# Attention on one core: the score products of two steps made together, with their low-key part on 64-row tiles

## The chip, the cores and the metric

The kernel runs on one core of one Trainium2 chip. The metric is the device time of one launch in microseconds; lower is better. A profiled execution is taken by the hardware profiler, and its page and trace are what is read here.

## The reference

The program is a small transformer layer in float32: half of a mixture-of-experts layer is added to x, then an attention block, then half of the same mixture-of-experts layer again. The change touches only the attention, with 4 sequences of 1024 tokens, width 256, 16 heads of 64:

```python
q = (_ln(x, lnq_s, lnq_b) @ Wq + bq).reshape(Bq, Sq, H, HD).transpose(0, 2, 1, 3)
k = ...   # the same with Wk, bk
v = ...
scores = jnp.einsum('bhqd,bhkd->bhqk', q, k) / SMAX
mask = jnp.triu(jnp.full((Sq, Sq), -999.0), k=Sq - 1)
p = jax.nn.softmax(scores + mask, axis=-1)
att = jnp.einsum('bhqk,bhkd->bhqd', p, v)
```

(Bq = 4, Sq = 1024, H = 16, HD = 64.)

## The kernel before

The whole program is one block in which each engine runs its own instruction stream, written out by hand, and the streams meet in semaphores. It has four phases: `ffn_phase`, `attention_phase`, `mlp_phase` and `ffn_phase` again. Float32 precision is kept by splitting each operand into a high and a low part in the type fp32r, and by multiplying the parts.

`attention_phase` works in steps. One step handles one tile of 128 queries of one head against all 1024 keys. Eight steps make a head, 16 steps a pair of heads (a "slot"), and 32 steps one iteration of the loop; 16 iterations make 512 steps. In step k of an iteration the engines do this:

- TensorE (PE), in `on_tensor`: four score matmuls into `sc[:, k % 2]` (L1675); then eight 128x128 transposes into `tr` of the tile of three steps ago (L1687); then four matmuls into `ov` for the values (L1711), which run seven steps behind the scores; then, where there is one, half of a projection piece, three matmuls' worth into `pj` (L1622, L1629), which makes queries, keys or values for a later slot.
- VectorE (DVE), in `on_vector`: where a block of values has ended, a copy to `half` (L1569); then the row maximum of the scores (L1578), in one step of eight after one small operation for the mask (L1575); the reciprocal of the last step's sum (L1583); and two subtractions that write the low part of the transposed probabilities into `pT` (L1589).
- ScalarE (ACT), in `on_scalar`: where a block has ended, a copy to `ao` (L1414); two copies that write the high part of the transposed probabilities (L1421); the exponential with its row sum (L1427); and, where there is a projection piece, a copy to `staged` (L1382, L1379).
- GpSimd (POOL), in `on_gpsimd`: the scaling by the reciprocal (L1505) and the splitting of staged queries, keys and values into parts (L1458 to L1484).

The plan `AT` puts a piece at the odd steps 1, 3, 5, 9, 17, 19, 21, 23, 25, 27, 29 and 31. Its first half runs in the even step ahead of it, so that the pairs of steps (0,1), (2,3), (4,5), (8,9) and all pairs from (16,17) have projections in both steps, and the pairs (6,7), (10,11), (12,13) and (14,15) have none. A block of values ends after every fourth step, so that `half` and `ao` are written in the steps 3, 7, 11, ... (the odd step of every second pair).

The scores of one step: `q_s[:, slot, head]` holds the high part of the head's queries on 64 partitions and the low part on the other 64. `k_s[:, slot, head, 0]` holds the high part of the keys on both halves, and `k_s[:, slot, head, 1]` the low part on both halves; the second half is written by a DMA on the SP queue (`double_k`, L1261). Two matmuls over all 128 rows, one for each of the two k parts, so give all four products for 512 keys, and four give a step's tile. `sc` has room for two tiles. Ahead of its score matmuls a step waits for the exponential of the tile of two steps ago (`pe.wait_ge(s["exp"], u - 1)`), which frees the place.

Of the kernel before, what the change touches and what calls it, by code (L numbers as in the profile page):

```python
# [20 lines left out]
F32 = mybir.dt.float32  # L21
# [1070 lines left out]
def attention_phase(nc, turns, tag, w, zT, w_split, bias, att):  # L1092
# [34 lines left out]
    q_s = m.sb("q_s", [P, 2, 2, S], F32R, room=rooms.first)  # L1127
    k_s = m.sb("k_s", [P, 2, 2, 2, S], F32R, room=rooms.first)
    pT = m.sb("pT", [P, 2, 2, QT, BT], F32R, room=rooms.wide)
# [100 lines left out]
    def after(it):  # L1230

        return (it + 1) % NIT

    def on_sync(sp, ahead):
# [23 lines left out]
        def double_k(slot):  # L1258

            for head, (a, b) in enumerate(((0, HD), (HD, 0))):  # L1260
                sp.dma_start(k_s[b:b + HD, slot, head].bitcast(F32), k_s[a:a + HD, slot, head].bitcast(F32))\  # L1261
                    .then_inc(s["k_dup"], 16)

        def double_first(part):
            cols = slice(part * BT, part * BT + BT)
            for head, (a, b) in enumerate(((0, HD), (HD, 0))):
                sp.dma_start(k_s[b:b + HD, 0, head, :, cols].bitcast(F32), k_s[a:a + HD, 0, head, :, cols].bitcast(F32))\
                    .then_inc(s["k_dup"], 16)
# [36 lines left out]
        def body(it, first, last):  # L1305
# [13 lines left out]
            if not ends(it):  # L1319
                sp.wait_ge(s["split"], before(it, PAIR_UP))  # L1320
                load_wqk(after(it), 0)
                load_z(after(it))
            else:
                sp.wait_ge(s["split"], before(it, PAIR_UP))
                ahead["loads"]()
            store(it, 0, it * 2 + 1)
# [6 lines left out]

            sp.wait_ge(s["split"], before(it, QUERIES_UP))
            load_wqk(after(it), 1)
            sp.wait_ge(s["split"], before(it, ITER))
# [6 lines left out]
        sp.wait_ge(s["z_in"], 32 * NIT)  # L1343
        sp.wait_ge(s["k_dup"], 32 * 2 * NIT + 32)
        sp.wait_ge(f["res_out"], NB * 16 + 16)
# [5 lines left out]
    def parts_of(kind, part, slot, pair_slot):  # L1351

        cols = slice(part * BT, part * BT + BT)
        r0, r1 = rows_of_head(0), rows_of_head(1)
        if kind == "Q":
            hi = [q_s[r0, pair_slot, 0, cols], q_s[r1, pair_slot, 1, cols]]
            lo = [q_s[r1, pair_slot, 0, cols], q_s[r0, pair_slot, 1, cols]]
        else:
            hi = [k_s[r0, pair_slot, 0, 0, cols], k_s[r1, pair_slot, 1, 0, cols]]
            lo = [k_s[r0, pair_slot, 0, 1, cols], k_s[r1, pair_slot, 1, 1, cols]]  # L1360
        return (staged[r0, slot], staged[r1, slot]), hi, lo

    def on_scalar(act, ahead):
# [80 lines left out]
    def on_gpsimd(pool, ahead):  # L1444
# [42 lines left out]
        for n, (kind, part) in enumerate(FIRST):  # L1487
# [8 lines left out]
            else:  # L1496

                (x0, _), hi, _ = parts_of(kind, part, n % 2, 0)
                pool.wait_ge(s["staged"], n + 1)
                pool.tensor_scalar(hi[0], x0, 1.0, 1.0, ALU.mult, ALU.mult).then_inc(s["head0_hi"], 1)  # L1500

# [103 lines left out]
    def on_tensor(pe, ahead):  # L1605
# [42 lines left out]
        def body(it, first, last):  # L1648
            for k in steps(last):
                u = it * ITER + k  # L1650
                slot, head, tile = k // STEPS, (k // QT) % 2, k % QT
                if not last:
# [5 lines left out]
                    if k % STEPS == 0:  # L1658

                        pe.wait_ge(s["k_dup"], it * 64 + slot * 32 + 64)  # L1660
                        if slot:
# [6 lines left out]
                    if first and k == 4:  # L1668
                        pe.wait_ge(s["first_split"], 4)
                    if not (first and k < 2):  # L1670

                        pe.wait_ge(s["exp"], u - 1)
                    for kb in range(S // BT):
                        for a in range(2):
                            o = pe.matmul(sc[:, k % 2, kb * BT:(kb + 1) * BT],  # L1675
                                          q_s[:, slot, head, tile * P:(tile + 1) * P],
                                          k_s[:, slot, head, a, kb * BT:(kb + 1) * BT],
                                          start=(a == 0), stop=(a == 1))
                    o.then_inc(s["sc"], 1)
                if transposes_at(k, first, last):  # L1680
# [588 lines left out]
```

## Time and profile before

| | us |
|---|---|
| median of 3 runs | 2418.85 (2418.18 to 2421.43) |
| the profiled execution's own time | 2419.73 |
| its span | 2417.9 |
| PE busy | 2377.2 (98%) |
| DVE busy | 1865.4 (77%) |
| ACT busy | 1680.0 (69%) |
| POOL busy | 1516.2 (63%) |

The attention takes the stretch from about 285 us to about 1965 us of the span. Busy time of PE is modelled: a matmul's record lasts longer than the distance to the next one, since they are pipelined. The distance from the start of one group of matmuls to the start of the next is the time that the group takes of PE.

### The profile page before, as it was taken

The page shows a single profiled execution, that of the slowest core. Times are in us where ns is not written, and L with a number is a line of the kernel's source. Part 1 is how long each engine was busy: PE and PEld are TensorE (multiplying, and loading weights), DVE is VectorE, ACT ScalarE, POOL GpSimd, SP SyncE. Part 2 cuts the span into 40 slices and gives each one's busy share as a digit, 9 for nine tenths or more (in the row PEclk, how much of TensorE's full clock was granted, in tenths as well). Part 3 has the DMA queues.
Part 4 walks back from the last instruction along what each step waited for, and adds up shares of the span by engine and source line. Part 5 has one row for each costly group of instructions (what it writes and reads, how often), then busy time and mean ns, then how long its engine had stood idle before and what let it go on. Part 6 is the DMA issues. An engine that isn't in the chain of part 4 may idle for free.

```text
span 2417.9 us, 46347 instructions
## 1 busy us (share of the span) xinstructions
PE 2377.2 (98%) x14512; PEld 2066.7 (85%) x14512; DVE 1865.4 (77%) x3615; ACT 1680.0 (69%) x2932; POOL 1516.2 (63%) x1536
## 2 busy tenths in 40 slices
PE   8999999999999999999999999999999999999999
PEld 7888878888888888888888888888888889988888
DVE  7887687888878788887878878788887875466775
ACT  4555677877878787787878878787787864443443
POOL 1333378787777877778787777878778754542220
PEclk9999999999999999999999999999999999999999
DMA  4744631322212232131223212122221345332332
GB/s 181 263 165 157 209 114 44 101 75 78 96 44 87 61 96 83 56 96 44 87 72 93 96 37 94 44 98 76 78 96 44 109 170 174 122 119 71 126 126 80
DMA packets 131970, 245.67 MB, mean 102 GB/s; under 512 B 7290, under 2 KB 90132, under 8 KB 120052
## 3 DMA queue, kind: packets, MB, share of 16 engines
q1 hardware_dynamic: 131828, 244.15, 30.9%
q8 instruction: 44, 0.72, 0.1%
q14 instruction: 98, 0.80, 0.1%
HBM read 140.12 MB, written 53.67 MB: 80 GB/s over the span
## 4 chain that ended last, share of the span: by engine, by line
PE 83%; DVE 7%; issue 4%; POOL 3%; DMA 2%; ACT 1%; SPq 0%; DVEq 0%; POOLq 0%; ACTq 0%
PE a_ov L1711 20%; PE a_sc L1675 19%; PE a_tr L1687 19%; PE a_pj L1622 7%; PE a_pj L1629 4%; PE g_acc L964 3%; PE g_hid L922 3%; PE f_acc L964 2%; PE f_hid L922 2%; PE m_proj L2125 1%; POOL m_zin L1971 1%; PE m_hid L2194 1%; DMA f_xin<-in_x 1%; DVE f_hp L736 1%; DVE f_gated L731 1%
## 5 line engine op out<-in xcount | busy, mean ns | idle before, releaser
L1578 DVE TENSOR_REDUCE a_nmax<-a_sc 128x1 f32<-128x1024 f32 x512 | 626.5, 1224 | 251.9 <-PE a_sc L1675 248.1
L1421 ACT ACTIVATE a_pT<-a_tr 128x512 fp32r<-128x512 f32 x1024 | 559.5, 596 | 317.2 <-PE a_tr L1687 307.7
L1505 POOL TENSOR_SCALAR a_pr<-a_pr,a_rden 128x1024 f32<-128x1024 f32 x512 | 576.3, 1127 | 283.4 <-DVE a_rden L1583 212.8
L1589 DVE TENSOR_TENSOR a_pT<-a_tr,a_pT 128x512 fp32r<-128x512 f32 x1024 | 649.2, 675 | 18.7 <-ACT a_pT L1421 18.7
L1711 PE MATMUL a_ov<-a_pT,a_v_s 128*128 128x512 f32 x2032 | 594.2, 414 | 1.6 <-DVE f_zT L778 1.2
L1427 ACT ACTIVATE a_pr<-a_sc,a_nmax 128x1024 f32<-128x1024 f32 x512 | 573.5, 1120 | 21.4 <-DVE a_nmax L1578 19.2
L1675 PE MATMUL a_sc<-a_k_s,a_q_s 128*128 128x512 f32 x2048 | 555.1, 393 | 0.5 <-DMA a_k_s<-a_k_s 0.5
L1687 PEld LDWEIGHTS a_tr<-f_ident,a_pr 128*128 128x128 f32 x4096 | 474.5, 140 | 82.8 <-DVE a_pT L1589 8.7
L1687 PE MATMUL a_tr<-f_ident,a_pr 128*128 128x128 f32 x4096 | 536.7, 273 | 3.5 <-DVE a_pT L1589 3.4
L1675 PEld LDWEIGHTS a_sc<-a_k_s,a_q_s 128*128 128x128 f32 x2048 | 375.6, 188 | 76.4 <-DMA a_k_s<-a_k_s 0.7
L1711 PEld LDWEIGHTS a_ov<-a_pT,a_v_s 128*128 128x128 f32 x2032 | 343.8, 189 | 47.9 <-issue 5.2
L1622 PE MATMUL a_pj<-a_z_s,a_wqk_s 128*128 128x512 f32 x756 | 213.7, 392 | 1.5 <-ACT a_staged L1382 1.1
L1622 PEld LDWEIGHTS a_pj<-a_z_s,a_wqk_s 128*128 128x128 f32 x756 | 141.4, 188 | 33.7 <-ACT a_staged L1382 1.4
L515 ACT ACTIVATE g_act_out<-g_hid,f_b 128x512 f32<-128x512 f32 x72 | 49.6, 689 | 129.9 <-PE g_hid L922 129.9
L964 PEld LDWEIGHTS f_acc<-f_w2p,f_hp 128*128 128x128 f32 x864 | 110.8, 190 | 19.5 <-DVE f_hp L736 14.6
L964 PE MATMUL f_acc<-f_w2p,f_hp 128*128 128x256 f32 x864 | 117.2, 285 | 7.5 <-DVE f_hp L736 7.3
L964 PEld LDWEIGHTS g_acc<-g_w2p,g_hp 128*128 128x128 f32 x864 | 111.4, 191 | 14.6 <-DVE g_hp L736 10.5
L964 PE MATMUL g_acc<-g_w2p,g_hp 128*128 128x256 f32 x864 | 116.3, 284 | 4.9 <-DVE g_hp L736 4.6
L1629 PEld LDWEIGHTS a_pj<-a_wv_s,a_z_s 128*128 128x128 f32 x756 | 105.8, 188 | 12.1 <-issue 0.7
L922 PE MATMUL f_hid<-f_xT,f_w1p 128*128 128x512 f32 x432 | 115.3, 403 | 0.0
L922 PE MATMUL g_hid<-g_xT,g_w1p 128*128 128x512 f32 x432 | 113.0, 397 | 0.0
L515 ACT ACTIVATE f_act_out<-f_hid,f_b 128x512 f32<-128x512 f32 x72 | 49.3, 685 | 90.9 <-PE f_hid L922 90.8
(265 smaller groups left out, 3236.3 us busy)
## 6 DMA issues: line engine op xcount, KB each, us to landing
a_z_s<-zT SPq DMA_DIRECT2D x32, 1024.0 KB, 7.7
a_k_s<-a_k_s SPq DMA_DIRECT2D x62, 512.0 KB, 5.7
a_wqk_s<-w_split SPq DMA_DIRECT2D x64, 256.0 KB, 3.1
a_v_s<-a_v_b SPq DMA_DIRECT2D x16, 1024.0 KB, 4.6
att<-a_ao SPq DMA_DIRECT2D x32, 512.0 KB, 2.9
m_in<-att SPq DMA_DIRECT2D x16, 1024.0 KB, 5.9
f_gB<-f_gate_rows SPq DMA_DIRECT2D x12, 1024.0 KB, 5.2
g_gB<-g_gate_rows SPq DMA_DIRECT2D x12, 1024.0 KB, 4.6
```

The source lines that it names most:

```text
L922: o = pe.matmul(hid[:, (par + e) % 2], w1p[:, a, (c * NE + x) * HID:(c * NE + x + 1) * HID], xT[:, par, c, b], start=(n == 0), stop=(n == 5))
L964: o = pe.matmul(acc[:, t], hp[:, e % 3, a, t * P:(t + 1) * P], w2p[:, b, x * D:(x + 1) * D], start=False, stop=(e == NE - 1 and (a, b) == ...
L1421: act.activation(pT[:, (u // 4) % 2, 0, 4 * part:4 * part + 4, (u % 4) * P:(u % 4 + 1) * P], tr[:, part].rearrange("p (t q) -> p t q", t=4 ...
L1427: act.activation(pr[:, k % NP], sc[:, k % 2], ACT.Exp, bias=nmax[:, k % NP:k % NP + 1], accum_out=den[:, k % NP:k % NP + 1]).then_inc(s["e ...
L1505: pool.tensor_scalar(pr[:, k % NP], pr[:, k % NP], rden[:, k % NP:k % NP + 1], 1.0, ALU.mult, ALU.mult).then_inc(s["normed"], 1)
L1578: dve.tensor_reduce(nmax[:, k % NP:k % NP + 1], sc[:, k % 2], AX.X, ALU.max, negate=True).then_inc(s["negmax"], 1)
L1589: dve.tensor_tensor(to[:, 1], tr[:, part].rearrange("p (t q) -> p t q", t=4), to[:, 0].bitcast(F32), ALU.subtract).then_inc(s["tr_lo"], 1)
L1622: o = pe.matmul(bank[:], wqk_s[:, "QK".index(kind), h, a], z_s[:, h * 2 + b, part], start=(h == 0 and i == 0), stop=(h == 1 and i == 2), s ...
L1629: o = pe.matmul(bank[:, h * 2 * P:(h + 1) * 2 * P], z_s[:, c * 2 + a, part // 2, col:col + P], wv_s[:, c, b], start=(i == 0), stop=(i == 5))
L1675: o = pe.matmul(sc[:, k % 2, kb * BT:(kb + 1) * BT], q_s[:, slot, head, tile * P:(tile + 1) * P], k_s[:, slot, head, a, kb * BT:(kb + 1) * ...
L1687: o = pe.transpose(tr[:, part, j * P:(j + 1) * P], pr[:, (k - LAG) % NP, (4 * part + j) * P:(4 * part + j + 1) * P], ident[:])
L1711: o = pe.matmul(values_bank(v, last)[:], v_s[:, vslot, kt, 2 * vhead:2 * vhead + 2] .rearrange("p k f -> p (k f)"), pT[:, blk % 2, a, kt], ...
```

## The change

Scores are made in the even steps alone, for two tiles at once. For each of the two tiles n, PE waits for the exponential of the tile that held `sc[:, n]` before, and does the two matmuls with the high keys over all 128 rows. Behind them come the low-key products of both tiles: four matmuls over 64 rows each, queries' high part times keys' low part alone. The two of one tile lie on different halves of the array's rows (keys 0 to 511 on rows 0 to 63, keys 512 to 1023 on rows 64 to 127). The product of the queries' low part with the keys' low part is no longer made. The rest of PE's order stays: transposes, values and projections of the even step, then those of the odd step.

The layout follows. `k_s` holds the doubled high keys of two heads, and in the place of the doubled low keys now `k_lo`, not doubled, with the two halves of the keys on the two halves of the partitions, and `q_x`, the queries' high part on the half of the partitions where `q_s` has the low part. `q_x` is written by a new pair of DMAs for each slot (`queries_across`), and `double_k` moves half as much as before. In the opening of the phase POOL writes `q_x` of the first slot, with two more operations for each of the two pieces of queries.

```diff
-    k_s = m.sb("k_s", [P, 2, 2, 2, S], F32R, room=rooms.first)
+    k_s = m.sb("k_s", [P, 2, 4, S], F32R, room=rooms.first)
+    k_lo = k_s[:, :, 2].rearrange("p s (h k) -> p s h k", h=2)
+    q_x = k_s[:, :, 3]
...
+        def queries_across(slot):
+
+            for head, (a, b) in enumerate(((0, HD), (HD, 0))):
+                sp.dma_start(q_x[b:b + HD, slot].bitcast(F32), q_s[a:a + HD, slot, head].bitcast(F32))\
+                    .then_inc(s["k_dup"], 16)
...
                 sp.wait_ge(s["split"], before(it, PAIR_UP))
+                queries_across(1)
                 load_wqk(after(it), 0)
                 load_z(after(it))
...
             sp.wait_ge(s["split"], before(it, QUERIES_UP))
+            queries_across(0)
             load_wqk(after(it), 1)
...
-            hi = [k_s[r0, pair_slot, 0, 0, cols], k_s[r1, pair_slot, 1, 0, cols]]
-            lo = [k_s[r0, pair_slot, 0, 1, cols], k_s[r1, pair_slot, 1, 1, cols]]
+            hi = [k_s[r0, pair_slot, 0, cols], k_s[r1, pair_slot, 1, cols]]
+
+            lo = [k_lo[rows_of_head(part), pair_slot, head] for head in range(2)]
...
+                if kind == "Q":
+                    for x, to in zip((x0, x1), across(part, 0)):
+                        pool.tensor_scalar(to, x, 1.0, 1.0, ALU.mult, ALU.mult)
...
-                        pe.wait_ge(s["k_dup"], it * 64 + slot * 32 + 64)
+                        pe.wait_ge(s["k_dup"], it * 128 + slot * 64 + 64)
...
-                    if not (first and k < 2):
-
-                        pe.wait_ge(s["exp"], u - 1)
-                    for kb in range(S // BT):
-                        for a in range(2):
-                            o = pe.matmul(sc[:, k % 2, kb * BT:(kb + 1) * BT],
-                                          q_s[:, slot, head, tile * P:(tile + 1) * P],
-                                          k_s[:, slot, head, a, kb * BT:(kb + 1) * BT],
-                                          start=(a == 0), stop=(a == 1))
-                    o.then_inc(s["sc"], 1)
+                    if k % 2 == 0:
+                        for n in range(2):
+                            if not (first and k == 0):
+
+                                pe.wait_ge(s["exp"], u - 1 + n)
+                            for kb in range(S // BT):
+                                pe.matmul(sc[:, n, kb * BT:(kb + 1) * BT],
+                                          q_s[:, slot, head, (tile + n) * P:(tile + n + 1) * P],
+                                          k_s[:, slot, head, kb * BT:(kb + 1) * BT], start=True, stop=False)
+                        for n in range(2):
+                            for kb in range(S // BT):
+
+                                r = rows_of_head(kb)
+                                q_hi = q_s[r, slot, head] if kb == head else q_x[r, slot]
+                                o = pe.matmul(sc[:, n, kb * BT:(kb + 1) * BT], q_hi[:, (tile + n) * P:(tile + n + 1) * P],
+                                              k_lo[r, slot, head], start=False, stop=True)
+                            o.then_inc(s["sc"], 1)
```

## Rows read from the trace of the kernel before

**Rows 1.** The page, part 2: the TensorE clock granted, in 40 slices

```profile
PEclk9999999999999999999999999999999999999999
```

**Rows 2.** Windows: us, then busy us (and instructions) of each engine, clock, DMA

```profile
800.00:1200.00 400.00, 399.90 (x2328) 341.26 (x2327) 327.41 (x538) 317.44 (x567) 303.27 (x312) 1.00 0.24 76
```

**Rows 3.** Groups by line from 900 to 1500 us: busy, mean ns | idle before

```profile
L1675 PE MATMUL a_sc<-a_k_s,a_q_s 128*128 128x512 f32 x737 | 199.6, 392 | 0.0
...
L1477 POOL TENSOR_SCALAR a_q_s<-a_staged 64x512 fp32r<-64x512 f32 x23 | 14.2, 619 | 1.9
```

**Rows 4.** Timeline of PE, one step with a projection, one without: start, us

```profile
1043.78 1.04 PE L1687 MATMUL a_tr<-f_ident,a_pr 128*128 128x128 f32 x8
1044.58 1.17 PE L1711 MATMUL a_ov<-a_pT,a_v_s 128*128 128x512 f32 x4
1045.59 0.85 PE L1622 MATMUL a_pj<-a_z_s,a_wqk_s 128*128 128x512 f32 x3
1046.28 1.08 PE L1675 MATMUL a_sc<-a_k_s,a_q_s 128*128 128x512 f32 x4
1047.20 1.03 PE L1687 MATMUL a_tr<-f_ident,a_pr 128*128 128x128 f32 x8
1047.99 1.17 PE L1711 MATMUL a_ov<-a_pT,a_v_s 128*128 128x512 f32 x4
1049.00 1.08 PE L1675 MATMUL a_sc<-a_k_s,a_q_s 128*128 128x512 f32 x4
1049.91 1.04 PE L1687 MATMUL a_tr<-f_ident,a_pr 128*128 128x128 f32 x8
```

**Rows 5.** Timeline of ACT in the same stretch

```profile
1044.42 1.08 ACT L1421 ACTIVATE a_pT<-a_tr 128x512 fp32r<-128x512 f32 x2 [1.21 <-PE a_tr L1687]
1045.39 1.12 ACT L1427 ACTIVATE a_pr<-a_sc,a_nmax 128x1024 f32<-128x1024 f32 x1
1046.39 0.21 ACT L1427 ACTIVATION_READ_ACCUMULATOR a_pr<-a_sc,a_nmax 128x1 f32 x1
1046.67 0.69 ACT L1382 ACTIVATE a_staged<-a_pj,f_bias 128x512 f32<-128x512 f32 x1
...
1050.04 0.68 ACT L1414 ACTIVATE a_ao<-a_ov,f_bias 64x512 f32<-64x512 f32 x1
1050.75 1.09 ACT L1421 ACTIVATE a_pT<-a_tr 128x512 fp32r<-128x512 f32 x2
```

**Rows 6.** Timeline of DVE in the same stretch

```profile
1043.98 1.22 DVE L1578 TENSOR_REDUCE a_nmax<-a_sc 128x1 f32<-128x1024 f32 x1 [0.91 <-PE a_sc L1675]
...
1045.20 1.27 DVE L1589 TENSOR_TENSOR a_pT<-a_tr,a_pT 128x512 fp32r<-128x512 f32 x2
...
1049.91 0.69 DVE L1569 COPY a_half<-a_ov 64x512 f32<-64x512 f32 x1
1050.63 1.23 DVE L1578 TENSOR_REDUCE a_nmax<-a_sc 128x1 f32<-128x1024 f32 x1
```

**Rows 7.** Timeline, first iteration: PE is released by a copy of ACT

```profile
308.53 0.69 ACT L1382 ACTIVATE a_staged<-a_pj,f_bias 128x512 f32<-128x512 f32 x1 [1.13 <-DVE f_bias L790]
...
309.26 0.53 PEld L1622 LDWEIGHTS a_pj<-a_z_s,a_wqk_s 128*128 128x128 f32 x3 [1.38 <-ACT a_staged L1382]
309.27 0.96 PE L1622 MATMUL a_pj<-a_z_s,a_wqk_s 128*128 128x512 f32 x3 [1.15 <-ACT a_staged L1382]
```

**Rows 8.** Timeline of ACT and PE where one iteration ends and the next begins

```profile
1025.81 0.60 ACT L1379 ACTIVATE a_staged<-a_pj 128x512 f32<-128x512 f32 x1
...
1026.53 1.03 PE L1687 MATMUL a_tr<-f_ident,a_pr 128*128 128x128 f32 x8
...
1028.57 1.09 ACT L1421 ACTIVATE a_pT<-a_tr 128x512 fp32r<-128x512 f32 x2 [2.17 <-PE a_tr L1687]
```

**Rows 9.** The page, part 6: issues, KB each, median us to landing

```profile
a_k_s<-a_k_s SPq DMA_DIRECT2D x62, 512.0 KB, 5.7
```

More of the change, by code:

```diff
@@ L1266, in double_first @@
             for head, (a, b) in enumerate(((0, HD), (HD, 0))):
-                sp.dma_start(k_s[b:b + HD, 0, head, :, cols].bitcast(F32), k_s[a:a + HD, 0, head, :, cols].bitcast(F32))\
+                sp.dma_start(k_s[b:b + HD, 0, head, cols].bitcast(F32), k_s[a:a + HD, 0, head, cols].bitcast(F32))\
                     .then_inc(s["k_dup"], 16)
@@ L1324, in body @@
                 sp.wait_ge(s["split"], before(it, PAIR_UP))
+                queries_across(1)
                 ahead["loads"]()
@@ L1343, in on_sync @@
         sp.wait_ge(s["z_in"], 32 * NIT)
-        sp.wait_ge(s["k_dup"], 32 * 2 * NIT + 32)
+        sp.wait_ge(s["k_dup"], 32 * 4 * NIT)
         sp.wait_ge(f["res_out"], NB * 16 + 16)
@@ L1358, in parts_of, with across @@
         else:
-            hi = [k_s[r0, pair_slot, 0, 0, cols], k_s[r1, pair_slot, 1, 0, cols]]
-            lo = [k_s[r0, pair_slot, 0, 1, cols], k_s[r1, pair_slot, 1, 1, cols]]
+            hi = [k_s[r0, pair_slot, 0, cols], k_s[r1, pair_slot, 1, cols]]
+            lo = [k_lo[rows_of_head(part), pair_slot, head] for head in range(2)]
         return (staged[r0, slot], staged[r1, slot]), hi, lo
+    def across(part, pair_slot):
+        cols = slice(part * BT, part * BT + BT)
+        return q_x[rows_of_head(1), pair_slot, cols], q_x[rows_of_head(0), pair_slot, cols]
     def on_scalar(act, ahead):
@@ L1496, in on_gpsimd @@
             else:
-                (x0, _), hi, _ = parts_of(kind, part, n % 2, 0)
+                (x0, x1), hi, _ = parts_of(kind, part, n % 2, 0)
                 pool.wait_ge(s["staged"], n + 1)
+                if kind == "Q":
+                    for x, to in zip((x0, x1), across(part, 0)):
+                        pool.tensor_scalar(to, x, 1.0, 1.0, ALU.mult, ALU.mult)
                 pool.tensor_scalar(hi[0], x0, 1.0, 1.0, ALU.mult, ALU.mult).then_inc(s["head0_hi"], 1)
```

## The prediction

> **What bounds the kernel now.** I read the page first, then the windows, the groups by line, and last the timeline of each engine through two neighbouring steps. The clock is at 2.4 GHz through the whole span, so nothing is to be won or explained there [rows 1]. In a 400 us window of the attention PE is busy 399.9 us, while DVE, ACT and POOL have 18 to 24% of their time free [rows 2], and the score matmuls show no idle time ahead of them [rows 3]. PE is the bound, and every nanosecond taken from it is a gain, but only as long as nobody else becomes late.
>
> The distances between starts give PE's price list [rows 4]: eight transposes 0.79 us, four value matmuls 1.01, half a projection 0.69, four score matmuls 0.92. That is 3.42 us for a step with a projection and 2.71 without. By 24 and 8 such steps an iteration is 103.8 us; counted, it is 104.2 (737 records are 184.25 steps in 600 us, 3.256 us each, times 32) [rows 3]. The missing 0.4 are small waits. I compare with 104.2.
>
> **What the change takes from PE.** One 512-column matmul costs 0.92 / 4 = 0.23 us [rows 4]. A pair of steps had eight, and now has four over 128 rows and four over 64 rows. If the two on different halves of the rows run side by side, the latter cost two places, not four. That saves 2 x 0.23 = 0.46 us a pair, 7.4 us an iteration, 118 us in 256 pairs. No row of before shows a matmul over 64 rows; bounds are 0.46 us for the four (side by side) and 0.92 (one after another). I take 0.46, since each of them is written to a bank and to rows of its own.
>
> **The mode change** happens twice a pair, in and out, and no row shows one. The floor is nothing. If the array must be empty first, the tail of the last matmul is uncovered: its record is 0.39 us long where the next one follows after 0.23 [rows 3, 4], so 0.16. If the next weight load also can't run ahead, its cold start comes on top, 0.96 - 0.85 = 0.11 us for the same three matmuls behind a wait and without one [rows 4, 7]. So 0, 0.16 or 0.27 each, and 0, 0.33 or 0.55 a pair. I take 0.33, the middle one, since it asks for an empty array and for nothing more. The Trainium skill (TensorEngine Tiling (Array Packing), Tiling Modes, Key Properties) says that a change of the tiling mode, not of the tile, drains TensorE; by that rule the free case is out, and 84 us (256 x 0.33) of the saving is gone. Another rule of the skill (TensorE: Matmul & The Clock Gate, Part 3, The mechanism) says that a weight load overlaps a running matmul only where their row groups differ or where it goes to the background buffer. By its first half the second tile's loads would be exposed, an estimated 0.11 a pair, some 28 us; the rows speak against that, since four matmuls over the same 128 rows follow one another at 0.23 us and only the first one behind a wait pays 0.11 [rows 4, 7].
>
> **The new wait is the main thing.** Before, step k waited for the exponential of tile k-2, which ACT had finished a step earlier. Now the second tile's high products, at the even step, wait for the exponential of the tile just before, k-1, whose turn on ACT comes behind the high copies of the transposes that PE made only in that same odd step. Behind this wait on PE stand the low products of both tiles, the transposes, values and projections; so DVE and ACT, which wait for scores, run dry in the meantime. I lay out a pair (k even, mode change first at nothing), from the moment 0 at which DVE can begin the maximum of tile k. That is 0.20 after the place of its last matmul on PE (scores at 1042.87 plus four places, DVE at 1043.98) [rows 4, 6]. PE's low products of tile k+1 take the 0.23 after tile k's, so transposes k-3 start at 0.03.
> - ACT: high copies 0.64 behind the transposes' start [rows 4, 5], at 0.67, 0.97 for both; exponential k at 1.64; ACT free 1.28 later, 2.92; the sum is read 1.21 after its start [rows 5].
> - DVE: low parts from 1.30 (first high copy done), 1.27 long; done 2.60 [rows 6].
> - In an odd step in which a block ends, ACT first copies to `ao` (0.71), then does the high copies of k-2 at 3.63, and exponential k+1 at 4.60. DVE, with `half` (0.72) and the maximum (1.22), comes to 4.57, so both are equally late [rows 5, 6]. Exponential k+1 is done at 5.81. PE is released 0.04 after such an end and pays 0.11 for the cold load [rows 7]: 5.96. Then high products 0.46, low ones of the first tile 0.23, and 0.20 to be seen: **6.85 us** for the pair, in 8 of 16 pairs, with or without a projection.
> - No block end, with projections (7 pairs): transposes k-2 start at 0.03 + 0.79 + 1.01 + 0.69 = 2.52; copies 3.16, exponential 4.13 to 5.34, next maximum at **6.38**. PE's own work is 2 x 3.42 - 0.46 = 6.38 too, so this pair has the whole gain.
> - Neither (one pair): copies at 2.92, exponential 3.89 to 5.10: **6.14**.
>
> Sum: 8 x 6.85 + 7 x 6.38 + 6.14 = 105.6 us. Before, the same pairs took 6.84 with projections and 5.42 without: the 0.46 is won in seven pairs of sixteen, nothing in the five where a block ends beside a projection, and the four without projections lose 0.7 to 1.4 each.
>
> **The turn of the loop.** ACT's first copy of an iteration comes 2.16 us behind the end of its last one, 26.41 to 28.57, about 1 us after the transposes were ready [rows 8]. Before, PE had a step's cover for that. Now the last pair's staging ends at 5.88 + 0.60 = 6.48, the first copy can start at 8.64, and it is wanted at 6.85 + 0.67 = 7.52: 1.12 late, right on the chain, less by what the mode changes delay the rest: 0.8 at 0.33.
>
> **The rest.** The two DMAs more for each slot move in sum what was moved before, since the doubling halves; a double takes 5.7 us to land [rows 9]. `queries_across` is released by the last piece of queries, in about step 11 and step 27, for use in steps 16 and 32, some 13 us ahead; what stands behind it on SP (weights, z) is wanted later still. POOL's two more operations for each of two pieces in the opening cost 4 x 0.62 us [rows 3], partly on the way to the first scores; I book 1.5 once. Costs of the split operations are the same, only their target rows differ.
>
> **The sum.** An iteration is 105.6 + 16 x 0.33 + 0.8 = 111.7 us, 7.5 more than 104.2. Sixteen give 120, plus 1.5: +121 us on a span of 2417.9 (the execution's own time is 2419.73, the median 2418.85, 1 us apart). **2540 us**, 5% slower. Mode changes lie on the chain in full, because nobody has work in hand while PE switches. With a free change: 105.6 + 1.1 = 106.7, +41, 2460. At 0.55: 105.6 + 8.8 + 0.6 = 115.0, +174, 2593.
>
> **The rivals.** What this kernel's measurement can tell from no change is about 0.2%, 5 us.
> - The forecast, mode change about 0.33 a pair: 2540, its own range 2500 to 2570. Chance 0.35.
> - Mode change nearly free: 2460. For it: PE goes from 512-column matmuls to transposes and back without an extra gap [rows 4]. Against it: neither of those alters how rows are grouped. Chance 0.20.
> - Mode change with uncovered loads: 2593. Chance 0.22.
> - **Faster.** The wait for the second exponential costs PE less than laid out, because ACT's chain is shorter; then PE's sum alone counts: -118 + 84 = -34, 2385. Its place is the wait ahead of the second tile's high products. It decides if that chain is 0.47 us a pair shorter than I have it, or 0.16 with a free mode change. ACT's 20% of free time speaks for it [rows 2]; that this time lies just where ACT waits for the next scores speaks against it. Chance 0.11.
> - The tiles don't run side by side: each tile's low products cost 0.23 more, both on the chain, +0.46 a pair, +118: 2658. Chance 0.08.
> - Gain and waits cancel: within 5 us of 2419. Chance 0.04.
>
> So faster 0.11, same 0.04, slower 0.85. The range is 2415 to 2615: it leaves out the faster case and the serial one, 0.19, and holds the bounds of the mode change.
>
> **What would show it.** In the trace after, PE should stand idle ahead of the score matmuls with ACT's exponential as its releaser, 0.1 us in seven pairs and up to 1.5 in pairs without projections; pairs with a block end should be alike, about 6.85 plus the mode change. DVE should wait for scores in even steps only, over 1.2 us a time. The mode change is the distance from the last high product to the first low one, less 0.23, and likewise to the transposes. The two low products of a tile should start within some ns; 0.23 apart would mean that they don't overlap. I am wrong if score waits are missing (then the saving shows), or if the clock falls from the level of rows 1.

## The result, and the profile after

| | before | after |
|---|---|---|
| median, us | 2418.51 (2417.19 to 2421.43, 4 runs) | 2545.86 (2544.87 to 2547.11, 4 runs) |
| ratio | | 1.0526, 95% interval 1.0513 to 1.0539 |
| span of the profiled execution, us | 2417.9 | 2543.8 |

The changed kernel is 127 us slower, 5.3%. The forecast was 2540, within 2415 to 2615. The range is wide, from no change to 8% slower, so it is the point and its terms that are held against the runs below.

The page of the kernel after, parts 1, 2 and 4: busy time, the clock granted, and the chain that ended last.

```profile
PE 2439.4 (96%) x14512; PEld 1913.1 (75%) x14512; DVE 1890.9 (74%) x3615; ACT 1670.6 (66%) x2932; POOL 1520.1 (60%) x1540
...
PEclk9999999999999999999999999999999999999999
...
PE 69%; DVE 9%; ACT 9%; issue 8%; POOL 2%; DMA 1%; SPq 0%; DVEq 0%; ACTq 0%; POOLq 0%
```

The clock is that of [rows 1]. PE does fewer places of matmul work (a place is the 0.23 us from one 512-column matmul to the next) and yet is busy for longer; its records overlap and their length is modelled. What counts is that DVE, ACT and "issue" (time in which an engine waits for nothing that the profile shows) now have 26% of the chain. Before they had 12%:

```profile
PE 83%; DVE 7%; issue 4%; POOL 3%; DMA 2%; ACT 1%; SPq 0%; DVEq 0%; POOLq 0%; ACTq 0%
```

The same 400 us window as in [rows 2]:

```profile
800.00:1200.00 400.00, 388.94 (x2201) 288.01 (x2200) 310.77 (x502) 295.30 (x532) 287.01 (x300) 1.00 0.22 66
```

Every engine gets less done in the same time: 502 instructions on DVE against 538, 532 on ACT against 567. PE is down from 399.9 us to 388.9, and no other engine is busier than before, as one would expect of a chain through several engines. The groups of score matmuls from 900 to 1500 us (busy, mean ns | idle before), to be held against [rows 3]:

```profile
L1696 PE MATMUL a_sc<-a_k_s,a_q_s 128*128 128x512 f32 x344 | 107.6, 413 | 13.7 <-ACT a_pr L1444 13.2
...
L1704 PE MATMUL a_sc<-a_k_s,a_q_s 64*128 64x512 f32 x172 | 62.8, 445 | 0.0
L1704 PE MATMUL a_sc<-a_k_s 64*128 64x512 f32 x172 | 62.8, 445 | 0.0
```

344 records of the high products are 86 pairs in 600 us: 6.98 us a pair, 111.6 an iteration. That count is rough, since the stretch does not end with a pair. From the first maximum of the second iteration to that of the sixteenth (timelines of DVE) it is 1566.4 us, 111.9 an iteration, and in the kernel before 1461.6, 104.4. The difference is the 7.5 of the forecast. The new releaser is there: PE stands idle for the exponential (L1444). Records hide part of an idle time; the list of waits in the same stretch (total us, times, longest) shows it on the weight loads:

```profile
PEld a_sc L1696 <- ACT a_pr L1444: 41.2, 84, 1.2
...
PEld a_sc L1704 <- issue: 31.5, 86, 0.4
PEld a_tr L1714 <- issue: 31.5, 86, 0.4
```

84 of 86 pairs wait for the exponential. Twice a pair PE waits 0.36 us for "issue", ahead of the first 64-row load and ahead of the transposes behind the last one: nothing in the trace releases it, and these are the two mode changes.

One pair without projections and with a block end, in order of time (start, us):

```profile
1211.44 0.18 PEld L1704 LDWEIGHTS a_sc<-a_k_s,a_q_s 64*128 64x128 f32 x1 [0.38 <-issue]
1211.44 0.50 PE L1704 MATMUL a_sc<-a_k_s,a_q_s 64*128 64x512 f32 x1
1211.44 0.50 PE L1704 MATMUL a_sc<-a_k_s 64*128 64x512 f32 x1
1211.78 0.39 PE L1704 MATMUL a_sc<-a_k_s,a_q_s 64*128 64x512 f32 x1
1211.78 0.39 PE L1704 MATMUL a_sc<-a_k_s 64*128 64x512 f32 x1
1211.98 1.22 DVE L1598 TENSOR_REDUCE a_nmax<-a_sc 128x1 f32<-128x1024 f32 x1 [1.53 <-PE a_sc L1704]
1212.10 0.85 PEld L1714 LDWEIGHTS a_tr<-f_ident,a_pr 128*128 128x128 f32 x8 [0.37 <-issue]
1212.11 1.09 PE L1714 MATMUL a_tr<-f_ident,a_pr 128*128 128x128 f32 x8
1212.80 1.09 ACT L1438 ACTIVATE a_pT<-a_tr 128x512 fp32r<-128x512 f32 x2 [1.34 <-PE a_tr L1714]
1212.95 1.17 PE L1738 MATMUL a_ov<-a_pT,a_v_s 128*128 128x512 f32 x4
...
1213.77 1.12 ACT L1444 ACTIVATE a_pr<-a_sc,a_nmax 128x1024 f32<-128x1024 f32 x1
...
1214.75 0.68 DVE L1589 COPY a_half<-a_ov 64x512 f32<-64x512 f32 x1
...
1215.00 0.68 ACT L1431 ACTIVATE a_ao<-a_ov,f_bias 64x512 f32<-64x512 f32 x1
1215.47 1.22 DVE L1598 TENSOR_REDUCE a_nmax<-a_sc 128x1 f32<-128x1024 f32 x1
1215.71 1.09 ACT L1438 ACTIVATE a_pT<-a_tr 128x512 fp32r<-128x512 f32 x2
...
1216.71 0.42 PEld L1696 LDWEIGHTS a_sc<-a_k_s,a_q_s 128*128 128x128 f32 x2
1216.82 1.11 ACT L1444 ACTIVATE a_pr<-a_sc,a_nmax 128x1024 f32<-128x1024 f32 x1
1216.95 0.62 PE L1696 MATMUL a_sc<-a_k_s,a_q_s 128*128 128x512 f32 x2
1217.83 0.19 ACT L1444 ACTIVATION_READ_ACCUMULATOR a_pr<-a_sc,a_nmax 128x1 f32 x1
1218.08 0.73 PE L1696 MATMUL a_sc<-a_k_s,a_q_s 128*128 128x512 f32 x2 [0.51 <-ACT a_pr L1444]
1218.74 0.50 PE L1704 MATMUL a_sc<-a_k_s 64*128 64x512 f32 x1
```

- The two low products of a tile start in the same 0.01 us: they run side by side.
- The weight loads (PEld) of the first low products and of the transposes start together with their matmuls, 1211.44 and 1212.10. The load of the high products starts 0.24 us ahead of them, 1216.71 against 1216.95.
- Moment 0 of the prediction is 1211.98. The copies of tile k-3 start at 0.82 (forecast 0.67 plus the change out), exponential k at 1.79 (1.64 plus it), the copy to `ao` at 3.02 (2.92), exponential k+1 at 4.84 (4.60), done 6.04 (5.81). PE goes on 0.06 later. The first low product is next at 6.76, and DVE starts again at 7.30.
- From 1211.44 to 1218.74 the pair takes 7.30 us. Before, such a pair was 2 x 2.71 = 5.42 by [rows 4].

The first low products of the next pairs of that iteration, (8,9) to (12,13), give the other kinds: 6.75 with projections and no block end (1218.74 to 1225.49), 7.21 with a block end again, and 6.44 with neither. The table further down has the means of all of them.

```profile
1225.49 0.50 PE L1704 MATMUL a_sc<-a_k_s 64*128 64x512 f32 x1
...
1232.70 0.50 PE L1704 MATMUL a_sc<-a_k_s 64*128 64x512 f32 x1
...
1239.14 0.50 PE L1704 MATMUL a_sc<-a_k_s 64*128 64x512 f32 x1
```

### The profile page after: what moved, and what is told of

It is laid out like the page before. It is cut to its first block, busy times and chain, and to the rows that moved or that the text cites. A ratio compares the mean times of both kernels' runs of the same rounds, so it can differ in the third digit from the quotient of the medians.

```text
span 2543.8 us, 46441 instructions
## 1 busy us (share of the span) xinstructions
PE 2439.4 (96%) x14512; PEld 1913.1 (75%) x14512; DVE 1890.9 (74%) x3615; ACT 1670.6 (66%) x2932; POOL 1520.1 (60%) x1540
## 4 chain that ended last, share of the span: by engine, by line
PE 69%; DVE 9%; ACT 9%; issue 8%; POOL 2%; DMA 1%; SPq 0%; DVEq 0%; ACTq 0%; POOLq 0%
PE a_tr L1714 15%; PE a_ov L1738 13%; PE a_sc L1696 10%; PE a_sc L1704 7%; PE a_pj L1642 6%; PE a_pj L1649 3%; ACT a_pT L1438 3%; ACT a_pr L1444 3%; PE g_acc L964 3%; PE g_hid L922 3%; PE f_acc L964 2%; PE f_hid L922 2%; DVE a_nmax L1598 2%; PE m_proj L2152 1%; DVE a_pT L1609 1%
## 5 line engine op out<-in xcount | busy, mean ns | idle before, releaser
L1609 DVE TENSOR_TENSOR a_pT<-a_tr,a_pT 128x512 fp32r<-128x512 f32 x1024 | 657.1, 684 | 42.7 <-ACT a_pT L1438 26.7
L1444 ACT ACTIVATE a_pr<-a_sc,a_nmax 128x1024 f32<-128x1024 f32 x512 | 573.2, 1119 | 21.6 <-DVE a_nmax L1598 20.0
L1714 PEld LDWEIGHTS a_tr<-f_ident,a_pr 128*128 128x128 f32 x4096 | 449.2, 141 | 161.4 <-issue 101.3
L1714 PE MATMUL a_tr<-f_ident,a_pr 128*128 128x128 f32 x4096 | 562.1, 278 | 5.5 <-DVE a_pT L1609 0.7
L1696 PE MATMUL a_sc<-a_k_s,a_q_s 128*128 128x512 f32 x1024 | 321.1, 413 | 45.8 <-ACT a_pr L1444 44.5
L1696 PEld LDWEIGHTS a_sc<-a_k_s,a_q_s 128*128 128x128 f32 x1024 | 168.7, 188 | 144.7 <-ACT a_pr L1444 127.4
L1704 PE MATMUL a_sc<-a_k_s,a_q_s 64*128 64x512 f32 x512 | 186.9, 445 | 0.0
L1704 PE MATMUL a_sc<-a_k_s 64*128 64x512 f32 x512 | 186.9, 445 | 0.0
```

The source lines that it names most:

```text
L1444: act.activation(pr[:, k % NP], sc[:, k % 2], ACT.Exp, bias=nmax[:, k % NP:k % NP + 1], accum_out=den[:, k % NP:k % NP + 1]).then_inc(s["e ...
L1609: dve.tensor_tensor(to[:, 1], tr[:, part].rearrange("p (t q) -> p t q", t=4), to[:, 0].bitcast(F32), ALU.subtract).then_inc(s["tr_lo"], 1)
L1696: pe.matmul(sc[:, n, kb * BT:(kb + 1) * BT], q_s[:, slot, head, (tile + n) * P:(tile + n + 1) * P], k_s[:, slot, head, kb * BT:(kb + 1) * ...
L1704: o = pe.matmul(sc[:, n, kb * BT:(kb + 1) * BT], q_hi[:, (tile + n) * P:(tile + n + 1) * P], k_lo[r, slot, head], start=False, stop=True)
L1714: o = pe.transpose(tr[:, part, j * P:(j + 1) * P], pr[:, (k - LAG) % NP, (4 * part + j) * P:(4 * part + j + 1) * P], ident[:])
```

## The experiments

The change has two halves, the order (two tiles together) and the 64-row tiles. The first two kernels do one each.

**The order alone**, on the kernel before:

```diff
-                    if not (first and k < 2):
-                        pe.wait_ge(s["exp"], u - 1)
-                    for kb in range(S // BT):
-                        for a in range(2):
...
+                    if k % 2 == 0:
+                        for a in range(2):
+                            for n in range(2):
+                                if a == 0 and not (first and k == 0):
+                                    pe.wait_ge(s["exp"], u - 1 + n)
+                                for kb in range(S // BT):
+                                    o = pe.matmul(sc[:, n, kb * BT:(kb + 1) * BT],
...
```

> The kernel before, with the scores of two steps made together in the even step (high keys of both tiles, then low keys of both), but all eight matmuls over 128 rows: no 64-row tiles, no mode change, the layout of before. Theory A (the wait for the exponential of the tile just before is a loss of its own): the same chain as in the prediction with 0.46 us instead of 0.23 for each tile's low products gives 7.31 us for a pair with a block end (8 of 16), 6.84 for one with projections and no block end (7), 6.60 for the one with neither, 113.0 an iteration, 114.1 with the turn of the loop, 9.9 over 104.2: +158, 2577 us. Theory B (the order costs nothing, all the loss is in the mode change): PE's work is that of before, 2419 us.

Measured: 2572.47 us, ratio 1.0639 (1.0621 to 1.0657). The order costs 154 us by itself, with no tile and no mode change in it. Its list of waits from 900 to 1500 us has the same line as the changed kernel's, of the same size:

```profile
PEld a_sc L1676 <- ACT a_pr L1427: 41.4, 82, 1.2
```

**The tiles alone**, on the changed kernel's layout:

```diff
-                    if k % 2 == 0:
-                        for n in range(2):
-                            if not (first and k == 0):
-                                pe.wait_ge(s["exp"], u - 1 + n)
...
+                    if not (first and k < 2):
+                        pe.wait_ge(s["exp"], u - 1)
+                    for kb in range(S // BT):
+                        pe.matmul(sc[:, k % 2, kb * BT:(kb + 1) * BT], ..., start=True, stop=False)
+                    for kb in range(S // BT):
+                        r = rows_of_head(kb)
...
```

> The changed kernel's layout and 64-row tiles, but each step makes its own scores (two high products, a mode change, two low products side by side, a mode change back) and waits for the exponential of two tiles ago as before. Twice as many mode changes as in the changed kernel. In its trace a pair with both mode changes costs 0.355 us more than the places of its matmuls. Theory A: PE stays the bound, each step gives 0.23 and pays 0.355, +0.125 in 512 steps: +64, 2483 us, so less than the changed kernel's 2546 although it changes mode twice as often. Theory B (mode changes are all the loss, (127 + 118) / 256 = 0.96 us a pair in the changed kernel): each step gives 0.23 and pays 0.96, +374, 2792 us.

Measured: 2479.15 us, ratio 1.0254 (1.0237 to 1.0271), 61 over before. One step without a projection, from PE's timeline:

```profile
1099.63 0.63 PE L1693 MATMUL a_sc<-a_k_s,a_q_s 128*128 128x512 f32 x2
1100.19 0.50 PE L1699 MATMUL a_sc<-a_k_s 64*128 64x512 f32 x1
1100.20 0.50 PE L1699 MATMUL a_sc<-a_k_s,a_q_s 64*128 64x512 f32 x1
1100.62 1.09 PE L1709 MATMUL a_tr<-f_ident,a_pr 128*128 128x128 f32 x8
1101.47 1.17 PE L1733 MATMUL a_ov<-a_pT,a_v_s 128*128 128x512 f32 x4
1102.49 0.63 PE L1693 MATMUL a_sc<-a_k_s,a_q_s 128*128 128x512 f32 x2
```

Here nothing waits, so the price of a mode change in and out can be read off. From the first high product to the first low one it is 0.56 us, where two places are 0.46: 0.10. From there to the transposes 0.43 or 0.42, where one place is 0.23: 0.20. From the transposes to the values 0.85, where [rows 4] have 0.79: 0.06. In sum 0.36 against a saving of 0.23 in a step, so that the step takes 2.86 us instead of 2.71 [rows 4]. With one mode change in and out a step, the tiles alone can only lose.

**No mode change**, all else as in the changed kernel. The low product of each tile is a single matmul over all 128 rows for the first 512 keys; that of the other keys is left out.

```diff
                         for n in range(2):
-                            for kb in range(S // BT):
-                                r = rows_of_head(kb)
-                                q_hi = q_s[r, slot, head] if kb == head else q_x[r, slot]
-                                o = pe.matmul(sc[:, n, kb * BT:(kb + 1) * BT], q_hi[...], k_lo[r, slot, head], ...)
+                            o = pe.matmul(sc[:, n, 0:BT], q_s[:, slot, head, (tile + n) * P:(tile + n + 1) * P],
+                                          k_lo[:, slot, head], start=False, stop=True)
```

> The changed kernel with one low product for each tile over all 128 rows in place of the two side by side over 64: it writes the first 512 keys alone, so the low product of the other 512 keys is left out (and this one adds a small product too many). PE's places are those of the changed kernel, without any mode change. Theory A: the mode change lies on the chain with its full 0.355 us a pair, 256 x 0.355 = 91 less, 2455 us, still 36 over before, since the wait for the exponential remains. Theory B (mode changes are all the loss): 118 under before, 2301 us.

Measured: 2463.65 us, ratio 1.0188 (1.0171 to 1.0205). That is 82 under the changed kernel, 0.32 us a pair on average, nine less than the 91 expected, and still 45 over before. The traces show where most of the nine are: fifteen pairs of an iteration are 0.34 to 0.37 us shorter than in the changed kernel (6.39 against 6.76, 6.95 against 7.30), but the first one takes 6.88 here and 6.87 there. At the turn of the loop ACT's late first copy holds the pair up, and the mode change costs nothing. That makes 5.6 us of the nine; the rest stays open. PE's timeline shows the places without a gap, 0.94 for four, 0.46 for two, and 0.79 for the transposes:

```profile
1099.85 1.10 PE L1696 MATMUL a_sc<-a_k_s,a_q_s 128*128 128x512 f32 x4
1100.79 0.62 PE L1700 MATMUL a_sc<-a_k_s,a_q_s 128*128 128x512 f32 x2
1101.25 1.03 PE L1710 MATMUL a_tr<-f_ident,a_pr 128*128 128x128 f32 x8
1102.04 1.17 PE L1734 MATMUL a_ov<-a_pT,a_v_s 128*128 128x512 f32 x4
```

Its idle time for the exponential is the changed kernel's: 12.5 us in the stretch where that has 13.2.

**Do the two products of a tile gain from lying on different rows?** All four low products on rows 0 to 63; the low product of the upper 512 keys is left out, and a small product of the first 512 keys is added in its place:

```diff
-                                r = rows_of_head(kb)
-                                q_hi = q_s[r, slot, head] if kb == head else q_x[r, slot]
+                                r = rows_of_head(0)
+                                q_hi = q_s[r, slot, head] if head == 0 else q_x[r, slot]
```

> The changed kernel with all four low products of a pair on rows 0 to 63, so that no two of them can run side by side; the product for keys 512 to 1023 takes its data from the first 512, so their low product is left out and a small wrong one is added. Mode changes, waits and instruction counts are those of the changed kernel. Theory A (two products on different rows share one place of 0.23 us): each tile's low products take 0.23 more, both lie on the chain, 256 x 0.46 = +118 on the changed kernel, 2664 us. Theory B (the two products don't gain from their rows, the 0.34 us between the tiles' products is the time of two): 2546 us.

Measured: 2663.69 us, ratio 1.101 (1.0992 to 1.1028), 118 over the changed kernel, which is 0.46 us a pair. PE's timeline has the four in a row, 1.12 us from the first to the transposes where the changed kernel has 0.67:

```profile
1099.85 1.19 PE L1704 MATMUL a_sc<-a_k_s 64*128 64x512 f32 x4
1100.97 1.09 PE L1714 MATMUL a_tr<-f_ident,a_pr 128*128 128x128 f32 x8
```

So the tiles do on PE what they are made for: two products in one place. The four start at 1099.85, 1100.19, 1100.42 and 1100.65 us: only the first, whose load starts with it, takes 0.11 more than a place. The loads behind it lie on the same rows as the product that is running and are hidden all the same. So the 28 us that the prediction weighed for the second tile's loads are not there.

**Is it the softmax between the scores that sets the pace?** The maximum and the exponential over the first 512 keys alone (but for the first four tiles), in the changed kernel and, as the control, in the kernel before. The other half of the softmax is left out.

```diff
-                    act.activation(pr[:, k % NP], sc[:, k % 2], ACT.Exp, ...)
+                    w = S if first and k < NP else BT
+                    act.activation(pr[:, k % NP, 0:w], sc[:, k % 2, 0:w], ACT.Exp, ...)
...
-                    dve.tensor_reduce(nmax[...], sc[:, k % 2], AX.X, ALU.max, ...)
+                    w = S if first and k < NP else BT
+                    dve.tensor_reduce(nmax[...], sc[:, k % 2, 0:w], AX.X, ALU.max, ...)
```

> The changed kernel with the row maximum and the exponential over the first 512 keys of each tile alone (but for the first four tiles); the other half of the softmax is left out. PE's instructions are all there. Theory A (the chain maximum, exponential, copies, exponential sets the pairs): maximum and exponential are each some 0.55 us shorter, the chain falls under PE's own work in all pairs with projections, 6.74 each with the mode changes, 6.1 and 5.5 without; 104.7 an iteration and some 0.5 for the turn: about 107 under the changed kernel, 2440 us. Theory B (PE is slow by itself, through mode changes or through the memory that the 64-row products read): 2546 as before.

> The control: the kernel before with the same half of the softmax left out. PE bounds it, so that both theories expect at most 6 us less (the 0.4 us of small waits in each iteration), 2413 to 2419 us.

Measured: 2456.99 us, ratio 1.0153 (1.0138 to 1.0169), and 2406.55 us, ratio 0.9948 (0.9933 to 0.9963). Work that is taken from DVE and ACT, none from PE, gives the changed kernel 89 us and the kernel before 13 (2419.75 in the same round). The control fell 6 us below what was expected, the changed kernel stayed 17 above. The idle time of the high products is gone, 0.1 us in place of 13.7 in the same stretch, and their weight loads wait 7.3 us for the exponential in place of 41.2:

```profile
L1698 PE MATMUL a_sc<-a_k_s,a_q_s 128*128 128x512 f32 x360 | 101.0, 397 | 0.1
```

The 17 us lie in the four pairs without projections. They were forecast at 6.1 and 5.5 us and took 6.45, 6.26, 6.26 and 6.01, 1.2 us an iteration more, although PE's own work in them is 5.42 - 0.46 + 0.36 = 5.32. Half a softmax less is not enough to free these pairs of the other engines.

**Another order**, an attempt to give the wait its cover back: in the even step the transposes go ahead of the scores on PE, and on DVE the low parts ahead of the maximum.

```diff
+                early = transposes_at(k, first, last) and not last and k % 2 == 0
+                if early:
+                    transposes_now()
...
+                for part_ in (reciprocal, lows, maximum) if k % 2 == 0 and not last else (maximum, reciprocal, lows):
+                    part_()
```

> The changed kernel with the even step's eight transposes ahead of the pair's scores on PE instead of behind them, and on DVE, in even steps, the reciprocal and the low parts ahead of the row maximum. ACT and DVE then have copies to do while PE makes the scores, and the wait for the second exponential gets 0.79 us more cover. Theory A: a pair with a block end comes to about 6.8 us with the mode change, one with projections alone to 6.74 (PE's own 6.38 + 0.355), the one with neither to 6.3: 107.9 an iteration, +60 on before, about 2480 us, 65 under the changed kernel. Theory B (the loss is not in the order): same as the changed kernel, 2546.

Measured: 2614.55 us, ratio 1.081 (1.0792 to 1.0828). My theory missed this by 135 us: slower than the changed kernel, not faster. The wait for the exponential is gone (the high products have no idle time), but others have come. In an odd step with a block end the values of the next block wait for `ao`, which ACT copies behind exponential k; with the transposes gone from the front, PE is there earlier. Pairs with a block end take 7.6 us on average (6.95 to 8.03):

```profile
1107.27 0.67 ACT L1431 ACTIVATE a_ao<-a_ov,f_bias 64x512 f32<-64x512 f32 x1
...
1107.99 1.19 PE L1749 MATMUL a_ov<-a_pT,a_v_s 128*128 128x512 f32 x4 [0.27 <-ACT a_ao L1431]
...
1124.61 1.20 PE L1749 MATMUL a_ov<-a_pT,a_v_s 128*128 128x512 f32 x4 [0.77 <-ACT a_ao L1431]
```

And at the turn of the loop, where the first pair takes 8.85 us, ACT's first copy comes 2.00 us behind its last one, 1110.53 to 1112.53, when PE's transposes have been ready since 1110.76 (timelines of ACT and of PE); DVE's low parts, now ahead of the maximum, pass that on to the maximum and so to the exponential, and the later transposes wait for them:

```profile
1109.93 0.60 ACT L1396 ACTIVATE a_staged<-a_pj 128x512 f32<-128x512 f32 x1
1112.53 1.09 ACT L1438 ACTIVATE a_pT<-a_tr 128x512 fp32r<-128x512 f32 x2 [2.01 <-issue]
```

```profile
1109.73 1.03 PE L1684 MATMUL a_tr<-f_ident,a_pr 128*128 128x128 f32 x8
...
1118.28 1.25 PE L1684 MATMUL a_tr<-f_ident,a_pr 128*128 128x128 f32 x8 [1.50 <-DVE a_pT L1612]
```

The longest wait in this kernel's list is ACT's for the maximum, 170 us in 82 times from 900 to 1500 us, where the changed kernel has 5. With the low parts ahead of it the maximum starts 0.5 to 1.0 us behind the pair's first low product, away from the turn, where the changed kernel has 0.54. The exponential k, which has no copies ahead of it any more, starts 1.8 to 2.3 us behind that product instead of 2.33, so little of the cover was won there. PE's order and DVE's order were changed in one kernel, so what each costs was not told apart.

The next kernel takes the first of these away: both copies of an ended block move into the even step in which it ends, on ACT ahead of the exponential, on DVE behind the low parts and the maximum.

```diff
-                v = finished_at(k, first)
...
+                v = ended_at(k, first)
```

> The kernel with the transposes first, and with the two copies of an ended block of values (to ao on ACT, to half on DVE) moved from the odd step into the even step in which the block ends: on ACT ahead of the exponential, on DVE behind the row maximum. In the trace of the kernel with the transposes first, pairs without a block end take 6.8 us as forecast, pairs with one 7.8, since PE waits for ao ahead of the next block's first product; and the first pair of an iteration takes 8.85, since ACT's first copy comes 2.0 us after its last one. Theory A (it is this copy): pairs with projections at 6.8, the others at 6.4, and 2.0 for the turn of the loop, 109.2 an iteration, about 2499 us. Theory B (something else in that order): 2615 us.

Measured: 2577.71 us, ratio 1.0653 (1.0637 to 1.067). It gives back 37 of the 116 us that I had put down to the copy. The wait for `ao` is no longer among the long ones; ACT now stands ahead of that copy for PE's values, 81 us in 42 steps of the same stretch, and the exponential behind it is late, with 62 us of PE's weight loads waiting for the low parts. The copy was a part of it: pairs with a block end are down from 7.6 to 7.28 us, not to 6.8 or 6.4, and the first pair of an iteration still takes 8.52. That the rest comes from the copy in its new place, ahead of the exponential, is what these waits suggest; no kernel here tests it.

**Does the moved copy help the kernel before?**

> The kernel before with the same two copies moved into the step in which the block ends. There PE waits 0.26 us for ao in one or two steps of an iteration. Theory A: 16 times 0.3, 2414 us. Theory B: the exponential comes later by the copy and is missed elsewhere: 2419 us or more.

Measured over 11 runs: 2419.55 us, ratio 1.0002 (0.9993 to 1.0011). The moved copy changes nothing, and Theory A's 2414 lies outside the interval. None of the kernels that do all the work beats the one before.

## Why the prediction was right, point by point

The two halves of the change and both together form a square: 2419 with neither, 2572 with the order, 2479 with the tiles, 2546 with both. The order is the larger loss. With it in place the tiles do help: 27 us less. In fifteen pairs of an iteration they give 0.46 us and the mode change takes 0.36 back, some 25 us in all; in the first pair of an iteration neither shows (6.88 us with the order alone, 6.87 with both).

The pairs of the changed kernel, by the distance between their first low products, as means over iterations 3 to 14:

| pair | number | forecast with the mode change, us | measured, us |
|---|---|---|---|
| with a block end | 8 | 7.18 | 7.26 (four at 7.30, four at 7.21) |
| projections, no block end | 6 | 6.71 | 6.76 |
| the same, first of the iteration | 1 | 6.71 + 0.8 | 6.87 |
| neither | 1 | 6.47 | 6.43 |
| an iteration | 16 | 111.7 | 111.9 |

- **What bounds before.** Right: half a softmax less gave it 13 us only, and its iteration then took 103.9 us, where the prediction's price list gives 103.8 for PE alone.
- **The saving on PE, 0.46 us a pair, 118 us.** Right in size. Putting the products on the same rows gave back just that, 118.
- **The mode change, 0.33 a pair.** It was 0.36 in the timeline and about 0.35 in each pair but the first of an iteration, where it was hidden; 0.32 on average. The forecast chose the sum well, not its parts. I had taken two uncovered tails of 0.16. Read off are 0.10 going in, 0.11 in the first product behind it (the second tile's product starts 0.34 after the first), 0.09 or 0.10 going out (0.32 or 0.33 from the last low product to the transposes, for a place of 0.23) and 0.06 in the first transpose. The load that comes first behind each change starts together with its matmul, as the rows of the pair show. So loads did not run ahead across the change, which I had in the dear case alone, and the tail costs less than its whole 0.16. The prediction's way of measuring it, the distance at each of the two edges less a place, gives 0.19 and misses the 0.11 and the 0.06 behind them. By the Trainium skill (TensorEngine Tiling (Array Packing), Tiling Modes, Key Properties) a mode change drains the engine; the trace agrees that it isn't free, with those numbers. The same section of the Trainium skill says that different tiles can run in parallel. The equal starts bear it out, and so do the 118 us that four products on the same rows cost.
- **The new wait.** Right, and the main thing. 6.85, 6.38 and 6.14 us plus 0.33 were forecast, 7.18, 6.71 and 6.47; measured are 7.30 or 7.21, 6.75 and 6.44. 84 of 86 pairs wait for the exponential, and DVE waits for scores once a pair, 86 times at 1.3 to 1.4 us on average, as the prediction said that it would show. Of the 0.12 missing in a pair at 7.30, 0.03 is the mode change; in the pair shown above, most of the rest arises before the second exponential, which starts at 4.84 where 4.60 and a change out of 0.15 give 4.75. There the two high copies take 1.11 us of ACT instead of 0.97. In the pairs at 7.21 the copy to `ao` takes 0.57 instead of 0.71, DVE is the later one, and the second exponential starts at 4.75. Why the copy is shorter for one of the two heads stays open. PE was released 0.06 after the exponential and its first two products took 0.11 more than without a wait, 0.73 against 0.62, as forecast from [rows 7].
- **No gain on a pair with a block end, a loss without projections.** Right: 7.3 against 6.84 and 5.42. In the trace before, pairs without projections took 5.5 to 5.7 us by the starts of their scores, so the loss in them is a little smaller than forecast.
- **The turn of the loop, 0.8 us.** Wrong in size: the first pair takes 0.11 us more than its kind, 6.87 against 6.76. ACT's gap, put at 2.16, is not one number. It was 1.83 to 2.14 us over the turns of the changed kernel and 1.97 to 2.27 in the kernel before. In the turn at 1190.42, with a gap of 1.84, the copy came 0.26 late and the pair still took 6.75. The step that failed is that this delay lies right on the chain. In a pair with projections and no block end the prediction's own table has ACT free at 2.92 and the next copies at 3.16, so ACT has 0.24 to spare, 0.32 in the trace.
- **The sum.** The pairs came out 0.9 us an iteration dearer than forecast and the turn 0.7 cheaper; that 111.9 is so near to 111.7 is partly luck.
- **The total, 2540 against 2546.** The sum takes all sixteen iterations as alike. The last one has 24 projection matmuls where the others have 96, so most of its pairs are of the kind that loses. From its first maximum to the end of the program the changed kernel takes 13.5 us more than the kernel before, 569.4 against 555.9, and not 7.5. That is the 6 us by which the forecast was short. The 1.5 us for POOL's operations in the opening are not seen: the first maximum starts at 288.9 us, before at 289.1, and over these kernels at 288.0 to 289.3.
- **The DMAs.** Not tried by themselves. In the page after, the doubled keys land in 3.7 us at 256 KB and the moved queries in 3.5, and all idle time ahead of the high products is put down to the exponential, none to a DMA. The tiles alone, which have all of them, came out 4 us under a sum that has nothing for them.

**The rivals.** "Faster" is out: its place was the wait, and 84 of 86 pairs wait there. "The tiles don't run side by side" was 2658; a kernel made to do that took 2664, so this case was sized rightly and is not what happened. "Mode change nearly free" was 2460, and the kernel without one took 2464. "Uncovered loads" was 2593, 47 too much: its mechanism is seen, the loads are uncovered, but a change in and out costs 0.36 and not the 0.55 that it adds up. "Gain and waits cancel" is out by 127 us.

Where I failed is in the use of the same reasoning for a new order: I followed the wait that I wanted to remove and not the copy of the ended block behind it, which became the first to be late.

## What to carry to other kernels

When two steps of a pipeline are done together on one engine, work out the chain from the last result back to the buffer that it frees, with every instruction that the other engines have queued between: here a wait for the last result but one became a wait for the last, and it cost more than the work saved, though all the others had about 20% of free time. Price a change of PE's tiling mode at about 0.36 us in and out and ask how many matmul places it saves; here it saves two of 0.23. A sum made from the timeline, pair by pair and kind by kind, came within 0.7% of the time for every kernel whose order was placed instruction by instruction. For the two kernels with the transposes first, which were not, it missed by 135 and 79 us. A new order needs a new table.

## What I had not expected of the hardware

- A mode change costs at several places, none of them large: 0.10 in, 0.11 in the first product behind it, 0.09 out, 0.06 in the first transpose behind it. The trace puts 0.36 us of idle time ahead of each of the two loads down to "issue".
- Over 64 rows two products that share a place cost the same 0.23 us as one over 128 rows, with both weight loads, and products on the same 64 rows follow one another at that distance too: four and the change out took 1.12 (four places, 0.11 in the first and 0.09 out).
- The time from ACT's last instruction of an iteration to its first of the next is not fixed, even within one kernel: 1.97 to 2.27 us before, 1.83 to 2.14 after. What it depends on stays open.
